# Local-attention layers in slots of two head groups instead of one

## The reference

```python
def attn_layer(x, Wqkv, qs, ksc, Wo):
    qkv = x @ Wqkv                                  # 128 -> 3 * 1024, 16 heads of 64
    q, k, v = (sh(q), sh(k), sh(v))
    q = l2norm(q) * qs
    k = l2norm(k) * ksc
    q = q * cos * scale + rotate_half(q) * sin * scale
    k = k * cos * inv + rotate_half(k) * sin * inv
    out = local_attention(q, k, v)                  # a token sees its 32-token window and the one before
    return out @ Wo

def ffn_layer(x, g, bln, W1, b1, W2, b2):
    xn = (x - mu) / jnp.sqrt(var + 1e-05) * g + bln
    a, gate = jnp.split(xn @ W1 + b1, 2, -1)        # 2 * 341
    return a * jax.nn.gelu(gate, approximate=False) @ W2 + b2

for i in range(6):
    x = attn_layer(shift_tokens(x), ...) + x
    x = ffn_layer(shift_tokens(x), ...) + x
```

## Time and profile before

| what | value |
|---|---|
| median of 3 runs | 2745.71 us (2742.29 to 2750.16) |
| profiled execution, its own time | 2736.72 us |
| span of its instructions | 2734.9 us |
| local layers, first to last exponential | 665.6 to 2377.9 us |
| mean granted TensorE clock | 0.973 of full |

### The profile page before, as it was taken

How to read it: one execution, slowest core, us unless ns; L and a number is a source line. 1 busy time by engine, 2 the same in 40 slices (tenths; PEclk the granted TensorE clock), 3 DMA queues, 4 the chain that set the end, 5 groups by cost and what they waited for, 6 DMA issues and landing times.

```text
span 2734.9 us, 98096 instructions
## 1 busy us (share of the span) xinstructions
PE 2519.4 (92%) x36165; PEld 1721.1 (63%) x36169; DVE 2095.3 (77%) x4531; ACT 1899.0 (69%) x6651; POOL 1778.8 (65%) x1605
## 2 busy tenths in 40 slices
PE   6989888888999999999999999999999999879999
PEld 4656544445666666666666666666666666648884
DVE  6777677767888888888888888888888888765644
ACT  3666666656878787878877888888888878633323
POOL 1666765544977787877787788778777777521210
PEclk8999989988999999999999999999999999989999
DMA  4000010002111211111111211121112111100000
GB/s 134 11 11 10 12 45 10 10 9 69 35 32 32 56 39 38 33 49 45 41 32 36 58 41 32 32 62 40 33 32 62 37 36 32 43 1 1 1 1 16
DMA packets 177425, 92.28 MB, mean 34 GB/s; under 512 B 40950, under 2 KB 173257, under 8 KB 176977
## 3 DMA queue, kind: packets, MB, share of 16 engines
q1 hardware_dynamic: 168352, 82.00, 11.7%
q0 software_dynamic: 8192, 4.21, 1.1%
q10 hardware_dynamic: 432, 0.07, 0.0%
HBM read 32.06 MB, written 3.76 MB: 13 GB/s over the span
## 4 chain that ended last, share of the span: by engine, by line
POOL 35%; PE 20%; issue 11%; DVE 7%; ACT 3%; DVEq 0%; POOLq 0%; SPq 0%; DMA 0%; ACTq 0%
POOL rs L1507 17%; POOL t_pair L1497 12%; POOL pr L1488 5%; PE bank L1115 2%; PE scores L1160 1%; PE bank L1171 1%; PE bank L1108 1%; PE bank L1799 1%; PE bank L1823 1%; PE bank L1200 1%; PE scores L1142 1%; ACT pr L1430 1%; PE bank L2056 1%; PE bank L1793 1%; DVE qr_pair L1342 1%
## 5 line engine op out<-in xcount | busy, mean ns | idle before, releaser
L1507 POOL TENSOR_TENSOR rs<-ssc,neg_half 128x8 f32<-128x8 f32 x384 | 648.5, 1689 | 32.6 <-DVE ssc L1378 32.6
L1497 POOL TENSOR_TENSOR t_pair<-qn_pair,tabs 128x512 f32<-128x512 f32 x384 | 489.2, 1274 | 13.3 <-DVE qn_pair L1362 11.0
L1430 ACT ACTIVATE pr<-scores,negmax 128x64 f32<-128x64 f32 x1536 | 463.5, 319 | 4.3 <-DVE negmax L1387 0.4
L1488 POOL TENSOR_TENSOR pr<-pr,rec 128x256 f32<-128x256 f32 x384 | 235.7, 614 | 329.7 <-DVE rec L1355 329.7
L1108 PE MATMUL bank<-wqk,xs 128*128 128x512 f32 x768 | 396.1, 598 | 4.8 <-DVE qn_pair L1362 3.6
L1011 POOL DMA_INDIRECT rg_win<-rg_images,share_down x256 | 255.2, 997 | 139.9 <-DVE rg_prod L950 84.4
L1424 ACT COPY vt<-bank 128x256 f32<-128x256 f32 x361 | 134.6, 373 | 278.0 <-PE bank L1171 240.5
L1430 ACT ACTIVATION_READ_ACCUMULATOR pr<-scores,negmax 128x1 f32 x1536 | 321.7, 209 | 0.0
L1115 PEld LDWEIGHTS bank<-ident,qr_pair 128*128 128x128 f32 x1536 | 180.0, 142 | 183.1 <-DVE qr_pair L1342 145.9
L1362 DVE TENSOR_TENSOR qn_pair<-bank,rs 128x512 f32<-128x512 f32 x384 | 260.6, 679 | 23.1 <-POOL rs L1507 22.7
L1342 DVE TENSOR_TENSOR qr_pair<-t_pair 128x512 f32<-128x512 f32 x384 | 264.9, 690 | 10.7 <-issue 0.7
(11 more groups left out here) (309 smaller groups left out, 5609.7 us busy)
## 6 DMA issues: line engine op xcount, KB each, us to landing
rg_prod<-vt SPq DMA_DIRECT2D x1536, 32.0 KB
wqk<-in_L_ffn_Wqkv SPq DMA_DIRECT2D x20, 256.0 KB
rg_win<-rg_images,share_down POOLq DMA_INDIRECT x256
wv<-in_L_ffn_Wqkv SPq DMA_DIRECT2D x20, 128.0 KB
wo<-in_L_ffn_Wo SPq DMA_DIRECT2D x20, 128.0 KB
w<-in_L_ffn_W SPq DMA_DIRECT2D x6, 341.0 KB
rg_images<-rg_prod SPq DMA_DIRECT2D x1, 1625.0 KB, 7.7
rg_images<-XT SPq DMA_DIRECT2D x16, 64.0 KB
```

What stands on the lines that cost most here:

```text
L1430: ex = act.activation(pr[t % 2][:, h * BAND:(h + 1) * BAND], sl_ps[:, h // 2, h % 2 * BAND:(h % 2 + 1) * BAND], ACT.Exp, bias=negmax[t % 2 ...
L1488: pool.tensor_tensor(p, p, over(rec[t % 2][:, :], [P, GH, BAND], 2), ALU.mult).then_inc(a.p_scaled, 1)
L1497: pool.tensor_tensor(t2[t % 2][:, :].rearrange("p (i h f e) -> p i h f e", i=2, h=GH, f=2), qn[t % 2][:, :].rearrange("p (i h f e) -> p i ...
L1507: pool.tensor_tensor(rs[t % 2][:, :], ssc[t % 2][:, :], neg_half[:, 0:8], ALU.pow)\
```

## The change

A slot now handles two head groups of one sequence. A layer has `LTICKS` = 32 ticks, six layers 192. In each slot:

- `queries` is two products of 128x512, one for the queries and one for the keys of eight heads. Squaring, summing, power and scaling run twice, once for each. `values` is one product of 128x512.
- The rotary sum and product of DVE, the `negmax`, the reciprocal, the scaling of probabilities, and the copies of `vt`, `pT` and `oT` each take both groups in one instruction of twice the size. ACT takes eight exponentials.
- The delays become `L_QKV`, `L_ROPE`, `L_SCORE`, `L_V`, `L_PROB`, `L_OUT`, `L_PROJ` = 1, 2, 2, 2, 3, 4, 5. Rotary sum, transposes and scores share a slot. Exponentials, reciprocal, scaling, the copy to `vt`, its four transfers, `turn_probs`, the copy to `pT` and `attend` share a slot.
- `project` runs once for a sequence, in every other slot, in two halves of four products. The feed-forward products take the remaining places, up to three in a slot (`ffn(u, 0)`, `ffn(u, 1)`, `ffn(u, 2)`); a chunk starts every 8 slots.
- `vt` has two buffers (of both groups) instead of three. The four transfers of a slot carry both groups, 64 KB each instead of 32 KB. Weights are loaded in fewer, larger transfers.

```diff
-LOCAL = DEPTH * TICKS
+LTICKS = TICKS // 2
+LOCAL = DEPTH * LTICKS
+SEQS = DEPTH * B
...
-L_QKV, L_ROPE, L_TURN, L_SCORE, L_V, L_EXP, L_PROB, L_PROJ = 1, 2, 3, 4, 4, 5, 6, 7
-FFN_FIRST, FFN_EVERY = TICKS // NCH + L_PROJ, TICKS // NCH
+L_QKV, L_ROPE, L_SCORE, L_V, L_PROB, L_OUT, L_PROJ = 1, 2, 2, 2, 3, 4, 5
+FFN_FIRST, FFN_EVERY = 12, LTICKS // NCH
...
-            for t in range(LOCAL + 32):
-                if live(t):
-                    near, far = vt[t % 3], vx[t % 2]
...
+            for t in range(LOCAL):
+                near, far = vt2[t % 2], vx[t % 2]
+                sp.wait_ge(a.v_moved, TICKS + t + 1)
+                sp.wait_ge(a.o_ready, TICKS + t - 1)
+                if t:
+                    sp.wait_ge(a.v_spread, 64 * t)
+                for to, half, key, a_pair in ((0, 0, WINDOW, 0), (0, 1, HD, 0), (HD, 0, WINDOW, 1), (HD, 1, 0, 1)):
+                    sp.dma_start(far[to:to + HD, :, half * P:(half + 1) * P],
+                                 near[key:key + BAND, :, a_pair * P:(a_pair + 1) * P]).then_inc(a.v_spread, 16)
...
             def slot(u):
+                b = projected(u)
                 if live(u - L_QKV):
-                    queries(u - L_QKV)
+                    queries(u - L_QKV, 0)
+                    queries(u - L_QKV, 1)
+                if b is not None:
+                    project(b, 0, u)
+                ffn(u, 0)
+                if live(u - L_ROPE):
+                    turn_queries(u - L_ROPE, 0)
+                    turn_queries(u - L_ROPE, 1)
                 if live(u - L_PROB):
-                    turn_probs(u - L_PROB, u)
...
+                    turn_probs(u - L_PROB)
+                if b is not None:
+                    project(b, 1, u)
+                ffn(u, 1)
                 if live(u - L_SCORE):
-                    score(u - L_SCORE, u)
+                    score(u - L_SCORE)
                 if live(u - L_PROB):
-                    attend(u - L_PROB, u)
+                    attend(u - L_PROB)
                 if live(u - L_V):
                     values(u - L_V)
-                if live(u - L_PROJ):
-                    project(u - L_PROJ)
+                ffn(u, 2)
...
             def slot(u):
-                t = u - L_EXP
-                if live(t) and not bursts(u - 1):
-                    act.wait_ge(a.v_ready, TICKS + t + 1)
-                    act.wait_ge(a.o_ready, TICKS + t - 2)
-                    act.wait_ge(a.v_spread, 64 * max(t - 2, 0))
-                    act.copy(vt[t % 3][:, :], vl_ps).then_inc(a.v_moved, 1)
+                t = u - L_PROB
                 if live(t):
                     act.wait_ge(a.negmax_ready, TICKS + t + 1)
                     act.wait_ge(a.pT_ready, TICKS + t - 1)
                     act.wait_ge(a.rec_ready, TICKS + t - 1)
-                    for h in range(GH):
+                    for h in range(2 * GH):
...
+                if live(u - L_OUT):
+                    move_out(u - L_OUT)
+                if live(u - L_QKV):
+                    squares(2 * (u - L_QKV))
                 if live(t):
...
+                    act.wait_ge(a.v_ready, TICKS + t + 1)
+                    act.wait_ge(a.o_ready, TICKS + t - 1)
+                    act.wait_ge(a.v_spread, 64 * max(t - 1, 0))
+                    act.copy(vt2[t % 2].rearrange("p x n -> p (x n)"), vl_ps[:, :]).then_inc(a.v_moved, 1)
+                if live(u - L_QKV):
+                    squares(2 * (u - L_QKV) + 1)
+                if live(u - L_ROPE):
+                    move_turned(2 * (u - L_ROPE))
+                    if not bursts(u):
+                        move_turned(2 * (u - L_ROPE) + 1)
+                if live(t) and not bursts(u):
                     act.wait_ge(a.pT_ready, TICKS + t + 1)
                     act.wait_ge(a.o_ready, TICKS + t - 1)
-                    act.copy(pT[t % 2][:, 0:GB], pTl_ps).then_inc(a.pT_moved, 1)
+                    act.copy(pT[t % 2][:, :], pTl_ps[:, :]).then_inc(a.pT_moved, 1)
```

More of the change, by code:

```diff
@@ L1177, in ffn, with projection_read @@
+            def projection_read(u):
+                pe.wait_ge(a.added, B + min((u - L_PROJ - 1) // 2 + 1, SEQS))
+            def ffn(u, j):
+                c = chunk_at(u, F_MEAN)
+                if c is not None and j == 0:
+                    projection_read(u)
                     pe.wait_ge(s.lf_shifted, 2 * (c + 1))
@@ L1222, in pe_local, with late @@
+                if c is not None:
+                    w = FCH[j][1]
+                    if j == 0:
+                        projection_read(u)
+                        pe.wait_ge(s.lf_gated, 3 * c + 3)
+                        pe.wait_ge(s.wffn_loaded, c // NCH * 48 + 48)
+                    mm = pe.matmul(ffn_ps[:, :], w2[0:w, j, :], hg[j][0:w, :], start=(j == 0), stop=(j == 2))
+                    if j == 2:
+                        mm.then_inc(s.lf_y, 1)
             pe.wait_ge(s.wqkv_loaded, 16 * 12)
+            def late(u, half):
+                for j in ((0, 1), (2,))[half]:
+                    ffn(u, j)
@@ L1259, in tables, with ffn @@
                         .then_inc(s.tables_ready, 1)
-            def ffn(c, step):
-                l = c // NCH
-                if step == F_MEAN:
+            def ffn(u, j):
+                c = chunk_at(u, F_MEAN)
+                if c is not None and j == 0:
                     dve.wait_ge(s.lf_mean, c + 1)
@@ L1268, in ffn @@
                     dve.tensor_tensor(xc[:, :], xf[c % 2][:, :], ffn_ps[:, :], ALU.subtract).then_inc(s.lf_centred, 1)
-                if step == F_VAR:
+                if c is not None and j == 2:
                     dve.wait_ge(s.lf_var, c + 1)
@@ L1273, in ffn @@
                     dve.tensor_scalar(xv[:, :], ffn_ps[:, 0:CH], LN_EPS, None, ALU.add).then_inc(s.lf_vareps, 1)
-                if step == F_SPREAD:
+                c = chunk_at(u, F_SPREAD)
+                if c is not None and j == 2:
+                    l = c // NCH
                     dve.wait_ge(s.lf_spread, c + 1)
@@ L1381, in slot @@
+                ffn(u, 1)
+                b = projected(u)
+                if b is not None:
+                    dve.wait_ge(a.y_ready, B + b + 1)
+                    at = slice(b % B * P, (b % B + 1) * P)
+                    dve.tensor_tensor(ZT[:, at], yl_ps, ZT[:, at], ALU.add).then_inc(a.added, 1)
+                if live(u - L_QKV):
+                    normed(2 * (u - L_QKV))
                 t = u - L_SCORE
@@ L1534, in local_at @@
         def local_at(n):
-            u = TAIL + n - LATE.start
-            return u if u < SLOTS else None
+            u, half = divmod(n - LATE.start, 2)
+            return (TAIL + u, half) if TAIL + u < SLOTS else None
         def gla_pe(pe, c, step):
@@ L1842, in late_pe @@
                 if local_at(n) is not None:
-                    local(local_at(n))
+                    local(*local_at(n))
                 if n == -1:
```

583 lines of the change are left out of this document (292 added, 291 removed).

## The result

The changed kernel takes 3062.7 us (median of 4 runs, 3059.6 to 3065.6), the kernel before 2747.9 on the same chip: the ratio is 1.115, with a 95% interval of 1.113 to 1.117. I had predicted 3030, 1% less, in a range of 2885 to 3195, and slower with 95%.

A forecast was written before the change was run, and what follows sets the result against it. PE looked like the bound, busy 92% of the span; in the changed kernel the slot's transfer loop decides: 10.15 us plus 0.3 for the clock, 191 slots of 10.45, +286 us, about 3030 us, range 2885 to 3195.

The forecast's parts named there:

- The loop of a slot: Exponentials, copies, transfers, `attend`, `negmax`, next exponentials in one slot that no other overlaps: 10.15 us against 8.94.
- clock term: Local layers: more PE idle time lowers its clock, adding 0.3 us a slot, bounds 0 and 1.6.
- D: Time from a transfer batch's first issue to all landed: 4.2 us with twice the data.
- What hides beside it: Rest of the slot beside the transfers: scores end at 6.9, landing at 8.2, 1.3 us of slack.
- Rival 1: Local layers: the clock oscillates and PE ends the slot, mean 12.0 us, about 3325 us in all; 8%.
- Rival 2: Slot: the batch lands before the scores end, slot 8.84 us, kernel faster at about 2724 us; 4%.
- it wins from D below 3.0: Condition of Rival 2: the changed kernel is faster if the batch lands within 3.0 us of first issue.
- Rival 3: Transfers: D is 3.75 with no clock term, slot 9.70 us, about 2888 us; lower end of the main case.
- The signs: What the profile after would show in slots, transfers, engine waits and busy shares if right, such as slots of 10 us or more.
- PE idle before the first product of `attend`, over 1 us each and 190 times: Sign of being right: PE waits ahead of `attend`, put down to the transfers from `vt`.
- Issues of one batch over 3 us: Sign of a wrong step, in SP's transfers: D would be mis-sized; the issue was left at 2.4 us.

The follow-up runs named there:

- e4: Changed kernel with VectorE's second scaling ahead of `negmax` instead of behind it: 2957.7 us, ratio 1.106 to the kernel before.
- e12: Changed kernel with GpSimd's scaling and its two rotary products made plain copies, leaving out those multiplications: 3020.1 us, ratio 1.103 to the kernel before.
- e1: Changed kernel without the four transfers of a slot and the waits for them (`attend` reads wrong rows, same shapes): 2934.5 us, ratio 1.100.
- e8: Changed kernel with one slot more between exponentials and `attend`, reciprocal behind the rotary sum, second scaling ahead of `negmax`: 2804.4 us, ratio 1.051.
- e9: e8 with the first squaring among the exponentials, first sum of squares ahead of the rotary sum, GpSimd's powers ahead of its scaling: 3024.9 us, ratio 1.105.
- e3: Changed kernel with ACT copying the values between the fourth and fifth exponential, so the transfers start sooner: 2843.9 us, ratio 1.065.

## Why the prediction came out right, and where it was not

- **The loop of a slot** (right). The copy of the values behind eight exponentials, four transfers, `attend`, `negmax`, the next exponentials: issue at 3.96 for 3.96; `attend` to `negmax` 1.03 for 1.18; `negmax` 0.69 for 0.68. Where this loop alone is left it gives 10.43 and 10.44 (e4, e12), and the sum without its clock term was 10.15.
- **D** (4.2, right with a small error). The mean is 4.36 in the changed kernel and 4.53 in e4, the median of the changed kernel 4.02. Twice the data added more than the 0.12 of the sum: without an `instruction` packet D went from 3.67 to 4.01, with one from 4.41 to 4.70. The means lie closer because 272 of 368 batches met such a packet before and 82 of 156 after; in e4 it was 115 of 156.
- **"What hides beside it"** is the step that failed. I had the scores at 6.9 and "1.3 us of slack"; they end at 8.57, and there is none. The terms: the sum was to be done at 3.9 and is done at 4.90, because GpSimd's second product takes 2.27 on average and ends at 2.9, where with the 1.27 of the first it would end at 1.9, and because the sum then takes 1.80 and not 1.2. From there to the end of the scores I had 3.0 us and it takes 3.7. What I read from the earlier trace rows were lengths of instructions that did not meet each other. Before, they did not: `qr_pair` took 690 ns and `t_pair` on GpSimd 1274 (groups of the kernel before, 650 to 2380 us):

```profile
L1497 POOL TENSOR_TENSOR t_pair<-qn_pair,tabs 128x512 f32<-128x512 f32 x384 | 489.2, 1274 | 13.3 <-DVE qn_pair L1362 11.0 <-issue 0.9
...
L1342 DVE TENSOR_TENSOR qr_pair<-t_pair 128x512 f32<-128x512 f32 x384 | 264.9, 690 | 10.7 <-issue 0.7
L1488 POOL TENSOR_TENSOR pr<-pr,rec 128x256 f32<-128x256 f32 x384 | 235.7, 614 | 329.7 <-DVE rec L1355 329.7
```

- The number hides this step: forecast and result are 33 us apart, 29 of them in the slots (10.60 for 10.45). The loop of the landing alone makes 10.43, the second chain adds the last 0.17. That chain, which I had called hidden, would alone have made a slot of 10.3 (e1), so that the time came out within 1% is partly luck.
- **The clock term**, 0.3 us a slot, is luck as well. The window's clock is 0.97 against 0.99, and 113 of 2025 us were at the lower level, but the part of the loop that is TensorE's, `attend` to `negmax`, took less than in the sum (1.03 for 1.18). No run shows a cost of 0.3 us; the term stood in the place of the longer D and of the second chain. Rival 1 (12.0 us a slot) did not come up in any of the thirteen kernels.
- **Rival 2** (the landing isn't late, 8.84 us) fails twice: the landing is at 8.3, and without it (e1) the slot is 10.31. The condition "it wins from D below 3.0" was wrong: no D would have won. **Rival 3** had D too short, by 0.6 on average and by 0.26 in its shortest batches.
- **The signs.** Transfers issued and landed, ACT idle until `negmax`, lower busy shares: seen. "PE idle before the first product of `attend`, over 1 us each and 190 times": not seen, 0.8 us in 125 slots, and this one row is what first showed the second chain. "Issues of one batch over 3 us": not seen either, they take 2.6 on average.

## What to carry to other kernels

When slots are merged to save fixed costs, write down each loop from one slot's first instruction to the next one's, and do so for every chain that ends in it: here two of nearly equal length, so that removing or shortening one gave 0.2 to 0.4 us of 1.66, and a third of 9.3 behind them. Look at the busy share of the engine that does the work first: at 96% for TensorE, merging had at most 0.4 us a pair to win, and it gave up the distance of 7 us between a copy to `vt` and its use, in which the transfers had been hidden. An estimate of "what is hidden" needs the same care as the chain on top of it, contention between VectorE and GpSimd included.

## What the runs showed of the hardware

**VectorE and GpSimd shut each other out.** A VectorE instruction with two tensors in SBUF (product, rotary sum) and GpSimd's product, scaling or copy, which read SBUF, do not run together. Of these the one that starts first takes its own time; the other is lengthened by about the rest of it. Sum 1.22 alone, 1.99 behind the scaling; scaling 1.04 alone, 1.95 behind the sum; GpSimd's product 1.27 and 2.31; VectorE's product 1.26 and 2.07 (mean of e8); a GpSimd copy with one input 0.61 and 1.53. VectorE's square sums (one input) stay at 0.68 in all kernels. The Trainium skill, page "SBUF — State Buffer", section "SBUF: two separate sides", calls this an exclusive lock that whichever starts first holds for its whole instruction, and names a VectorE operation with two SBUF inputs against a GpSimd operation that reads SBUF. The trace agrees in each of these five pairs, and e12 is the case that shows the clause on GpSimd's side.

**GpSimd's power is an exception to who wins.** In e9 a power of 8 columns meets the rotary sum in each of 177 slots. In 92 of them the power starts first, by 0.5 us or more, and the sum still takes its own 1.21. The power then takes 1.64, its own time, in 48 cases and 3.23 in 44; behind the sum it takes 2.63. So "whichever starts first" does not hold for it, and what decides between 1.64 and 3.23 stays open (the profile's lengths on GpSimd are rough).

**Batches of transfers land late when an `instruction` packet is in flight.** Four transfers with 256 KB in all take 4.01 us from first issue to landed when no such packet meets them, four with half of that 3.67. With one the means are 4.70 and 4.41, and the longest 5.9 and 5.7. The place in the slot matters as well: moving its issue forward by 2.2 us (e3) moved the landing by 2.5, and at the early place fewer batches met such a packet (58 of 156 for 82), of which only one took over 4.7 us (41 before the move). Why so few of them are long there the runs don't tell.
